# Attention head sums: PSUM leaves by ScalarE and is added on GpSimd in place of VectorE

## The chip, the cores and the metric

The kernel runs on one core of one Trainium2 chip. The metric is the device time of one execution in microseconds (us), median of several runs. Lower is better.

## What is computed

A post-norm transformer layer on x of shape (4, 1024, 128): causal attention with 8 heads of width 128 and rotary positions, then a gated feed-forward net with two further hidden layers. The part that matters here:

```python
q = rope(einsum('btm,mhd->bthd', x, w_aq))
k = rope(einsum('btm,mhd->bthd', x, w_ak))
v = einsum('btm,mhd->bthd', x, w_av)
s = einsum('bihd,bjhd->bhij', q, k) / 128      # masked where i < j
p = softmax(s, axis=-1)
o = einsum('bhij,bjhd->bihd', p, v)
r = einsum('bihd,hdm->bim', o, w_ao)           # the sum over heads
x = layernorm(x + r)
```

## The kernel before, in words

Output and value weights are multiplied together once, so that each head's weighted values are already its share of `r`, and the sum over the 8 heads of a batch entry is a plain sum into `rT`, a tile of 128 x 4096 in SBUF. There are 32 heads in all (4 batch entries of 8), taken in pairs; each head has 1024 tokens, that is 8 score blocks of 128 queries (`ib` 0 to 7, block `ib` having 128 x (ib + 1) columns) and 2 chunks of 512 tokens.

Float32 operands are split for TensorE into a high part and a low part, and each product is three matmuls. The low part is a subtraction on VectorE or GpSimd, after the high part has been rounded by a copy.

Each engine runs its own program, written out by hand as 8 steps for each head (the functions `step`), and the programs meet only through semaphores. Within an engine the order is fixed: an instruction that waits holds up all behind it. In step s of a head:

- TensorE makes the scores of block s + 2 (L391 to L395), transposes the normalised probabilities of block s (L404, s + 1 transposes), projects queries and keys of the next head in steps 0 and 2, values of the pair in steps 4 to 6 of the even head (L311), and multiplies probabilities by values (`attend`, L311): chunk 0 of this head in steps 6 and 7, chunk 1 of the **previous** head in steps 1, 2 and 3 (6, 6 and 12 matmuls). Both chunks use the one PSUM bank `pv_ps`.
- VectorE takes the reciprocal of the row sums of block s + 1 (L635), adds up rotated tiles (`rope_sum`, L660, two SBUF inputs), takes the negative maximum of block s + 2 (L629), adds a finished chunk of the previous head to `rT` (L678, `add_head`, chunk 0 in step 0, chunk 1 in step 4), and forms the low parts (L645, L665).
- ScalarE exponentiates block s + 1 (L525), rounds rotated tiles (L556), copies the transposed blocks of s (L537), copies projections out (L548) and rounds values (L563).
- GpSimd normalises the probabilities of block s + 1 (L720), multiplies swapped halves by the sine (L725, steps 1 to 4) and forms the low part of the rotated tiles (L732, steps 3, 4, 6 and 0).

`attend` may overwrite the bank only when the chunk before has been added (semaphore `pv_added`), and `add_head` waits for `pv_done`, the end of a chunk's products. A short queue of transfers on SyncE swaps the halves of projections. The feed-forward net follows after the attention part, at about 792 us.

Of the kernel before, what the change touches and what calls it, by code (L numbers as in the profile page):

```python
# [20 lines left out]
ACT = mybir.ActivationFunctionType  # L21
# [6 lines left out]
P = 128  # L28
# [27 lines left out]
V_STEP = (4, 5, 6, 6)  # L56
PV0_PIECES = {6: range(0, 2), 7: range(2, 4)}
PV1_PIECES = {1: range(0, 2), 2: range(2, 4), 3: range(4, 8)}
ADD0_STEP, ADD1_STEP = 0, 4
LEND1 = (6, 7, 0)  # L60
LEND3 = (1, 2)
FILLS_OF = [1 if i < 4 else 2 for i in range(NI)]
# [57 lines left out]
def attention(nc, ctx, sem, rT, ident, x_split, qk_split, v_split, xT, w_q, w_k, w_vT, w_o, rope_in, ident_in, mask_in,  # L120
              ffn_raw, ffn_weights, ffn_loaded):

    def sb(name, shape, dt=F32, where=ctx):
        return where.enter_context(nc.sbuf_tensor(name, shape, dt))
# [8 lines left out]
    proj = sb("proj", [P, 2, BANK])  # L133
    by_cos = sb("by_cos", [P, NQK, BANK])
    swapped = sb("swapped", [P, NQK, BANK])


    pre = ExitStack()
# [51 lines left out]
    v_high = (sem("v_high"), NV)  # L190
    v_low = (sem("v_low"), NV)
    pv_done = (sem("pv_done"), CHUNKS)
    pv_added = (sem("pv_added"), CHUNKS)
    swap_done = [(sem("swap_done0"), 64), (sem("swap_done1"), 64)]
    w_staged = [(sem("w_staged0"), 16), (sem("w_staged1"), 16)]
# [14 lines left out]
    def number(head):  # L210
        return 2 * head[0] + head[1]
# [7 lines left out]
    def exists(head):  # L219
        n = number(head)  # L220
        return not isinstance(n, int) or 0 <= n < HEADS

    def wait_for(eng, signal, head, nth):


        semaphore, each = signal
        if exists(head):
            eng.wait_ge(semaphore, each * number(head) + nth + 1)
# [9 lines left out]
    def earlier(head, nth, by, each):  # L238

        return step_on(head, (nth - by) // each), (nth - by) % each  # L240
# [33 lines left out]
    def is_first(head):  # L274
        return isinstance(head[0], int) and number(head) == 0
# [38 lines left out]
    with nc.Block() as block:  # L314
# [63 lines left out]
        def _(pe):  # L378
# [60 lines left out]
            def attend(head, chunk, key_blocks):  # L439

                if key_blocks[0] == 0:
                    wait_for(pe, t_low, head, NT - 1 if chunk else 3)
                    pair = head[0] + head[1] // 2
                    wait_for_pair(pe, v_low, pair, NV - 1 if chunk else 1)
                    wait_for(pe, pv_added, *earlier(head, chunk, 1, CHUNKS))
                for jb in key_blocks:
                    i0 = max(0, jb * P - chunk * BANK)
                    last = split_products(pv_ps[:, i0:], [vals[:, part, jb, parity(head)] for part in range(2)],
                                          [pT[chunk][:, part, jb, i0:] for part in range(2)],
                                          jb == 0, jb == 4 * chunk + 3)  # L450
                if key_blocks[-1] == 4 * chunk + 3:
                    last.then_inc(pv_done[0], 1)
# [30 lines left out]
        def _(act):  # L483
# [75 lines left out]
            def values_high(pair, nth):  # L559
                wait_for_pair(act, v_projected, pair, nth)  # L560
                if nth == 0:
                    wait_for(act, pv_done, (pair, -1), 1)
                nc.scalar.activation(vals[:, 0, 2 * nth:2 * nth + 2].rearrange("p j q m -> p (j q m)"),  # L563
                                     bank("v", 0, nth), ACT.Copy).then_inc(v_high[0], 1)

            def step(head, s, b):
                ahead = step_on(head, (s + 1) // NI)
                if before_first(head) and s == 1:
                    act.wait_ge(vo_ready, 1)
                    nc.scalar.activation(v_parts[:, 0], vo_ps, ACT.Copy).then_inc(vo_high, 1)  # L570
                if before_first(head) and s == 4:
                    for b in range(1, B):
                        high_of_x(b)
                if before_first(head) and s == NI - 2:
                    save_weights()
                if before_first(head) and s == NI - 1:
                    act.wait_ge(vo_low, 1)
                    act.wait_ge(x_low, B)
                    act.wait_ge(masks_ready, 1)
                if is_first(head) and s == NI - 1:  # L580
                    for b in range(2, B):
                        save_x(b)
                if is_first(head) and s == 4:
                    act.wait_ge(w_saved, W_SAVED)
                    act.wait_ge(wv_staged, 16)
                if exists(ahead):
                    exponentiate(ahead, (s + 1) % NI)
                for target, j in rope_tasks(head, s, HIGH_STEP):
                    roped_high(target, j)
                if exists(head):  # L590
                    transposed_high(head, s)
                for target, j in rope_tasks(head, s, QK_STEP):
                    copy_projected(target, j)
                for c in v_tasks(head, s):
                    values_high(head[0], c)
# [4 lines left out]
        def _(dve):  # L600
# [64 lines left out]
                nc.vector.tensor_tensor(low, bank("v", 0, nth), high.bitcast(F32),  # L665
                                        ALU.subtract).then_inc(v_low[0], 1)

            def add_head(head, chunk):

                if not exists(head):  # L670
                    return
                col = number(head) // H * T + chunk * BANK
                acc = rT[:, bass.ds(col, BANK)] if not isinstance(col, int) else rT[:, col:col + BANK]
                if is_first(head):
                    dve.wait_ge(r_zero, 1)
                wait_for(dve, pv_done, head, chunk)
                wait_for(dve, pv_added, *earlier(head, chunk, 2, CHUNKS))
                nc.vector.tensor_tensor(acc, pv_ps[:], acc, ALU.add).then_inc(pv_added[0], 1)  # L678

            def step(head, s, b):  # L680
                if before_first(head) and s == 3:
                    dve.wait_ge(vo_high, 1)
                    nc.vector.tensor_tensor(v_parts[:, 1], vo_ps, v_parts[:, 0].bitcast(F32),
                                            ALU.subtract).then_inc(vo_low, 1)
                    nc.vector.tensor_copy(ident_b[:], ident[:])
                    nc.vector.tensor_copy(mask_b[:], mask_f[:]).then_inc(masks_ready, 1)
                if before_first(head) and s == 5:
                    for b in range(1, B):
                        low_of_x(b)
                if exists(step_on(head, (s + 1) // NI)):  # L690
                    inverse_sum(step_on(head, (s + 1) // NI), (s + 1) % NI)
                for target, j in rope_tasks(head, s, SUM_STEP):
                    rope_sum(target, j)
                if exists(step_on(head, (s + 2) // NI)):
                    negative_max(step_on(head, (s + 2) // NI), (s + 2) % NI)
                if s == ADD0_STEP:
                    add_head(step_on(head, -1), 0)
                if s == ADD1_STEP:
                    add_head(step_on(head, -1), 1)
                if exists(head):  # L700
                    transposed_low(head, s)
                for target, j in rope_tasks(head, s, COS_STEP):
                    times_cos(target, j)
                for c in v_tasks(head, s):
                    values_low(head[0], c)
# [3 lines left out]
        @block.gpsimd  # L709
        def _(pool):  # L710
            nc.gpsimd.memset(warm[:], 0.0).then_inc(warm_zero, 1)
            nc.gpsimd.memset(rT[:], 0.0).then_inc(r_zero, 1)
            pool.wait_ge(consts_loaded, 48)

            def normalize(head, ib):
                n = parity(head) * NI + ib
                wait_for(pool, inv_ready, head, ib)
                pool.sem_inc(pool_passed, 1)
                p = probs[:, ib % 4, :(ib + 1) * P]
                nc.gpsimd.tensor_scalar(p, p, inv_sum[:, n:n + 1], 1.0, ALU.mult, ALU.mult).then_inc(probs_ready[0], 1)  # L720

            def times_sin(head, j):
                c = ROPE_TILES[j][1]
                wait_for_swap(pool, head, j)
                nc.gpsimd.tensor_tensor(swapped[:, j], swapped[:, j], rope[:, 1, c * BANK:(c + 1) * BANK],  # L725
                                        ALU.mult).then_inc(sin_done[0], 1)

            def roped_low(head, j):
                which, c = ROPE_TILES[j]
                high, low = (qk[:, parity(head), which, part, c * BANK:(c + 1) * BANK] for part in range(2))  # L730
                wait_for(pool, rope_high, head, j)
                nc.gpsimd.tensor_tensor(low, swapped[:, j], high.bitcast(F32), ALU.subtract).then_inc(rope_low[0], 1)  # L732

            def step(head, s, b):
                ahead = step_on(head, (s + 1) // NI)
                if exists(ahead):
                    normalize(ahead, (s + 1) % NI)
                for target, j in rope_tasks(head, s, SIN_STEP):
                    times_sin(target, j)
                for target, j in rope_tasks(head, s, LOW_STEP):  # L740
                    roped_low(target, j)

            run_pairs(pool, step)


# [456 lines left out]
```

## Time and profile before

| what | before |
|---|---|
| median of 3 runs | 1084.09 us (1081.2 to 1084.93) |
| the profiled execution, time | 1084.27 us |
| the profiled execution, span | 1082.5 us |
| TensorE busy | 1000.0 us (92%) |
| VectorE busy | 852.7 us (79%) |
| ScalarE busy | 657.0 us (61%) |
| GpSimd busy | 584.8 us (54%) |
| mean granted TensorE clock | 0.976 of full speed |

Busy shares are means over two parts that differ: GpSimd works almost only in the attention part, TensorE in both. To see what one more instruction costs, the timelines of the engines at the same place have to be laid beside each other.

### The profile page before, as it was taken

The numbers are of one execution on the slowest core, as the hardware profiler recorded it, in microseconds if no ns is written. First come the engines' busy times: TensorE is split into PE (matmuls) and PEld (weight loads), VectorE is DVE, ScalarE is ACT, GpSimd is POOL, SyncE is SP. The second block draws the span as 40 slices with busy tenths as digits, with TensorE's granted clock in tenths as the row PEclk, the third lists the DMA queues.
The fourth block names the chain that finished last, engine by engine and source line by source line (L and its number), as shares of the span: only waits on it lengthen the run. The fifth ranks groups of instructions, "written<-read, shape, count | busy, mean of one in ns | idle before, by whom it ended". The sixth has DMA issues, their size and how long they took to land. (4 is left out here: it accounts for less than half of the span.)

```text
span 1082.5 us, 20027 instructions
## 1 busy us (share of the span) xinstructions
PE 1000.0 (92%) x5648; PEld 829.6 (77%) x5648; DVE 852.7 (79%) x1803; ACT 657.0 (61%) x1383; POOL 584.8 (54%) x536
## 2 busy tenths in 40 slices
PE   2799999999999999999999999999929999999995
PEld 1588788878878888887888888787727878788784
DVE  4888888988878898897989888888755668486744
ACT  4577776777767777776767777677625252343531
POOL 3676777777767777777787776778450101000000
PEclk8899999999999999999999999999969999999998
DMA  7542223532222323222222223231020000000000
GB/s 247 166 137 60 63 63 87 156 88 59 59 60 67 78 58 88 59 61 67 68 67 58 50 59 73 59 80 42 1 79 1 1 1 21 0 19 0 1 20 20
DMA packets 33292, 66.16 MB, mean 61 GB/s; under 512 B 5456, under 2 KB 6992, under 8 KB 32208
## 3 DMA queue, kind: packets, MB, share of 16 engines
q1 hardware_dynamic: 30400, 58.62, 20.4%
q10 hardware_dynamic: 2832, 6.82, 1.7%
q8 instruction: 29, 0.48, 0.2%
q14 instruction: 31, 0.25, 0.1%
HBM read 24.26 MB, written 7.34 MB: 29 GB/s over the span
## 5 line engine op out<-in xcount | busy, mean ns | idle before, releaser
L720 POOL TENSOR_SCALAR probs<-probs,inv_sum 128x128 f32<-128x128 f32 (+7 forms) x256 | 236.2, 923 | 177.9 <-DVE inv_sum L635 177.9
L537 ACT ACTIVATE pT<-psum 128x512 fp32r<-128x512 f32 (+3 forms) x384 | 176.1, 490 | 129.8 <-PE psum L404 128.7
L311 PE MATMUL psum<-pT,vals 128*128 128x512 f32 (+3 forms) x1152 | 243.5, 351 | 1.6 <-DVE rT L678 1.6
L525 ACT ACTIVATE probs<-psum,neg_max 128x128 f32<-128x128 f32 (+7 forms) x256 | 190.5, 744 | 57.3 <-DVE neg_max L629 55.6
L645 DVE TENSOR_TENSOR pT<-psum,pT 128x512 fp32r<-128x512 f32 (+3 forms) x384 | 199.9, 547 | 15.1 <-ACT pT L537 12.0
L311 PEld LDWEIGHTS psum<-pT,vals 128*128 128x128 f32 x1152 | 188.9, 190 | 23.6 <-DVE pT L645 1.7
L629 DVE TENSOR_REDUCE neg_max<-psum 128x1 f32<-128x128 f32 (+7 forms) x256 | 190.4, 744 | 6.3 <-PE psum L395 6.3
L404 PE MATMUL psum<-ident,probs 128*128 128x128 f32 x1152 | 175.8, 278 | 15.0 <-POOL probs L720 7.6
L725 POOL TENSOR_TENSOR swapped<-swapped,rope 128x512 f32<-128x512 f32 x128 | 166.2, 1299 | 39.5 <-DMA swapped<-proj 38.6
L901 PE MATMUL ps<-hid,w 128*128 128x512 f32 x768 | 181.3, 396 | 0.0
L901 PEld LDWEIGHTS ps<-hid,w 128*128 128x128 f32 x768 | 143.7, 188 | 34.5
L732 POOL TENSOR_TENSOR qk<-swapped,qk 128x512 fp32r<-128x512 f32 x128 | 166.1, 1298 | 2.8 <-ACT qk L556 2.8
L404 PEld LDWEIGHTS psum<-ident,probs 128*128 128x128 f32 x1152 | 134.5, 141 | 42.1 <-DVE pT L645 13.1
L391 PE MATMUL psum<-qk 128*128 128x384 f32 (+5 forms) x384 | 136.7, 356 | 25.8 <-POOL qk L732 22.9
L660 DVE TENSOR_TENSOR swapped<-by_cos,swapped 128x512 f32<-128x512 f32 x128 | 123.1, 963 | 44.9 <-POOL swapped L725 44.9
L394 PE MATMUL psum<-qk 128*128 128x384 f32 (+5 forms) x384 | 151.3, 394 | 0.0
L395 PE MATMUL psum<-qk 128*128 128x384 f32 (+5 forms) x384 | 131.8, 343 | 0.0
L311 PE MATMUL psum<-x_moving,w_stage 128*128 128x512 f32 (+1 forms) x384 | 106.7, 414 | 9.9 <-DVEq L622 9.9
L995 ACT ACTIVATE value<-ps,scales 128x512 f32<-128x512 f32 x64 | 43.5, 690 | 96.9 <-PE ps L901 96.5
L391 PEld LDWEIGHTS psum<-qk 128*128 128x128 f32 x384 | 73.0, 190 | 36.0 <-issue 26.8
L1026 POOL COPY y<-y_norm 128x512 f32<-128x512 f32 (+1 forms) x8 | 5.2, 653 | 166.3 <-DVE y_norm L1083 166.3
L548 ACT ACTIVATE proj<-psum 128x512 f32<-128x512 f32 x128 | 75.2, 600 | 30.8 <-PE psum L311 26.1
(78 smaller groups left out, 1246.5 us busy)
## 6 DMA issues: line engine op xcount, KB each, us to landing
swapped<-proj SPq DMA_DIRECT2D x256, 128.0 KB, 2.3
w_stage<-qk_split SPq DMA_DIRECT2D x30, 256.0 KB, 2.7
wv_stage<-v_split SPq DMA_DIRECT2D x15, 256.0 KB, 2.6
x_split<-ffn_raw ACTq DMA_DIRECT2D x2, 1024.0 KB, 5.9
ffn_raw<-g SPq DMA_DIRECT2D x2, 1024.0 KB, 8.2
x_moving<-x_split SPq DMA_DIRECT2D x2, 1024.0 KB, 6.0
out<-y SPq DMA_DIRECT2D x4, 512.0 KB, 2.6
raw_x<-xT SPq DMA_DIRECT2D x3, 512.0 KB, 11.5
```

Of the source, the lines that this page charges most:

```text
L311: ins = nc.tensor.matmul(out_ap, left[a], right[b], start=first and i == 0, stop=last and i == 2)
L391: nc.tensor.matmul(dst, left[0], right[0], start=True, stop=False)
L394: nc.tensor.matmul(dst, left[0], right[1], start=False, stop=False)
L404: last = nc.tensor.transpose(bank("t", head[1], nth)[:, (jb % 4) * P:(jb % 4 + 1) * P], probs[:, ib % 4, jb * P:(jb + 1) * P], ident[:])
L525: nc.scalar.activation(probs[:, ib % 4, :width].rearrange("p (h c) -> p h c", h=halves), score_ps[:, ib % 2, :halves, :half], ACT.Exp, bia ...
L537: nc.scalar.activation(pT[chunk][:, 0, 4 * f:4 * f + n_blocks, (ib % 4) * P:(ib % 4 + 1) * P], bank("t", head[1], nth)[:, :n_blocks * P].r ...
L629: nc.vector.tensor_reduce(neg_max[:, n:n + 1], score_ps[:, ib % 2, :halves, :half], AX.XY, ALU.max, negate=True).then_inc(max_ready[0], 1)
L645: nc.vector.tensor_tensor(low, bank("t", head[1], nth)[:, :n_blocks * P].rearrange("p (j i) -> p j i", i=P), high.bitcast(F32), ALU.subtra ...
L720: nc.gpsimd.tensor_scalar(p, p, inv_sum[:, n:n + 1], 1.0, ALU.mult, ALU.mult).then_inc(probs_ready[0], 1)
L725: nc.gpsimd.tensor_tensor(swapped[:, j], swapped[:, j], rope[:, 1, c * BANK:(c + 1) * BANK], ALU.mult).then_inc(sin_done[0], 1)
L732: nc.gpsimd.tensor_tensor(low, swapped[:, j], high.bitcast(F32), ALU.subtract).then_inc(rope_low[0], 1)
L901: last = nc.tensor.matmul(ps[:, c, o], w_at(base, a, k * HID, o * P), hid[:, c, layer, b, k], start=k == 0 and i == 0, stop=k == HT - 1 an ...
```

## The change

The add into `rT` moves from VectorE to GpSimd. GpSimd cannot read the bank here, so ScalarE first copies `pv_ps` into a new SBUF tile `pv_stage` (128 x 512, one buffer). TensorE may overwrite the bank once the copy is done (`pv_staged`), and the copy waits until the add before it has read the stage.

```diff
-ADD0_STEP, ADD1_STEP = 0, 4
+STAGE_STEP = (0, 4)
...
+    pv_stage = sb("pv_stage", [P, BANK])
...
+    pv_staged = (sem("pv_staged"), CHUNKS)
...
-                    wait_for(pe, pv_added, *earlier(head, chunk, 1, CHUNKS))
+                    wait_for(pe, pv_staged, *earlier(head, chunk, 1, CHUNKS))
...
+            def stage_head(head, chunk):
+                wait_for(act, pv_done, head, chunk)
+                wait_for(act, pv_added, *earlier(head, chunk, 1, CHUNKS))
+                nc.scalar.activation(pv_stage[:], pv_ps, ACT.Copy).then_inc(pv_staged[0], 1)
...
+                if s in STAGE_STEP and exists(step_on(head, -1)):
+                    stage_head(step_on(head, -1), STAGE_STEP.index(s))
                 if exists(ahead):
                     exponentiate(ahead, (s + 1) % NI)
...
-                if s == ADD0_STEP:
-                    add_head(step_on(head, -1), 0)
-                if s == ADD1_STEP:
-                    add_head(step_on(head, -1), 1)
...
+            def add_head(head, chunk):
+                col = number(head) // H * T + chunk * BANK
+                acc = rT[:, bass.ds(col, BANK)] if not isinstance(col, int) else rT[:, col:col + BANK]
+                if is_first(head) and chunk == 0:
+                    pool.wait_ge(r_zero, 1)
+                wait_for(pool, pv_added, *earlier(head, chunk, 2, CHUNKS))
+                wait_for(pool, pv_staged, head, chunk)
+                nc.gpsimd.tensor_tensor(acc, pv_stage[:], acc, ALU.add).then_inc(pv_added[0], 1)
...
                 for target, j in rope_tasks(head, s, LOW_STEP):
                     roped_low(target, j)
+                if s in STAGE_STEP and exists(step_on(head, -1)):
+                    add_head(step_on(head, -1), STAGE_STEP.index(s))
```

On ScalarE, steps 3 to 5 of an odd head read as follows before (`probs` rows are the exponentials, `qk<-swapped` the rounding of a rotated tile, `pT` the copies of transposed blocks):

```order
L525 ACTIVATE probs,row_sum<-psum,neg_max 128x640
L556 ACTIVATE qk<-swapped 128x512
L537 ACTIVATE pT<-psum 128x4x128
L525 ACTIVATE probs,row_sum<-psum,neg_max 128x768
L556 ACTIVATE qk<-swapped 128x512
L537 ACTIVATE pT<-psum 128x4x128
L537 ACTIVATE pT<-psum 128x128
L525 ACTIVATE probs,row_sum<-psum,neg_max 128x896
```

With the change the same stretch of ScalarE, the line numbers of the changed file being a little higher, is:

```order
L527 ACTIVATE probs,row_sum<-psum,neg_max 128x640
L558 ACTIVATE qk<-swapped 128x512
L539 ACTIVATE pT<-psum 128x4x128
L571 ACTIVATE pv_stage<-psum 128x512
L527 ACTIVATE probs,row_sum<-psum,neg_max 128x768
L558 ACTIVATE qk<-swapped 128x512
L539 ACTIVATE pT<-psum 128x4x128
L539 ACTIVATE pT<-psum 128x128
L527 ACTIVATE probs,row_sum<-psum,neg_max 128x896
```

The copy of the finished bank stands directly ahead of the exponential of block 5 (128x768), and waits there for the previous head's last products.

On GpSimd, steps 3 to 6 of the same head read before (`probs` rows are normalisations, `swapped` the sine products, `qk<-swapped,qk` the low parts):

```order
L720 TENSOR_SCALAR probs<-probs,inv_sum 128x640
L725 TENSOR_TENSOR swapped<-swapped,rope 128x512
L732 TENSOR_TENSOR qk<-swapped,qk 128x512
L720 TENSOR_SCALAR probs<-probs,inv_sum 128x768
L725 TENSOR_TENSOR swapped<-swapped,rope 128x512
L732 TENSOR_TENSOR qk<-swapped,qk 128x512
L720 TENSOR_SCALAR probs<-probs,inv_sum 128x896
```

With the change, the same stretch of GpSimd is:

```order
L713 TENSOR_SCALAR probs<-probs,inv_sum 128x640
L718 TENSOR_TENSOR swapped<-swapped,rope 128x512
L725 TENSOR_TENSOR qk<-swapped,qk 128x512
L713 TENSOR_SCALAR probs<-probs,inv_sum 128x768
L718 TENSOR_TENSOR swapped<-swapped,rope 128x512
L725 TENSOR_TENSOR qk<-swapped,qk 128x512
L734 TENSOR_TENSOR rT<-pv_stage,rT 128x512
L713 TENSOR_SCALAR probs<-probs,inv_sum 128x896
```

The add stands between the low part of the second rotated tile and the normalisation of block 6 (128x896).

## Rows read from the trace of the kernel before

**Rows 1.** Busy time by windows: from:to, us, busy (instructions), granted clock, DMA, GB/s

```profile
core 0: us, PE busy (x) PEld busy (x) DVE busy (x) ACT busy (x) POOL busy (x), PEclk, DMA share, GB/s
60.00:780.00 720.00, 698.65 (x4276) 587.05 (x4275) 621.28 (x1221) 513.97 (x1159) 529.03 (x487) 1.00 0.27 69
```

**Rows 2.** Waits of TensorE, 100 to 780 us: total, times, longest

```profile
PE psum L391 <- POOL qk L732: 9.5, 14, 0.7
PE psum L404 <- POOL probs L720: 4.9, 15, 0.4
PE psum L404 <- DVE pT L645: 4.8, 14, 0.7
```

**Rows 3.** Timeline of TensorE, head 15: start, duration, instructions, idle before

```profile
400.60 2.11 PE L311 MATMUL psum<-pT,vals 128*128 128x512 f32 x12
...
407.95 0.32 PE L391 MATMUL psum<-qk 128*128 128x128 f32 x1 [0.70 <-POOL qk L732]
...
408.87 0.98 PE L404 MATMUL psum<-ident,probs 128*128 128x128 f32 x7 [0.30 <-POOL probs L720]
```

**Rows 4.** Timeline of TensorE, head 16 and the start of 17

```profile
423.12 2.11 PE L311 MATMUL psum<-pT,vals 128*128 128x512 f32 x12
...
431.25 1.05 PE L404 MATMUL psum<-ident,probs 128*128 128x128 f32 x7
...
442.44 0.49 PE L404 MATMUL psum<-ident,probs 128*128 128x128 f32 x3
```

**Rows 5.** Timeline of ScalarE, head 16

```profile
424.09 0.90 ACT L525 ACTIVATE probs<-psum,neg_max 128x768 f32<-128x768 f32 x1
...
427.92 0.60 ACT L563 ACTIVATE vals<-psum 128x512 fp32r<-128x512 f32 x1
428.42 1.00 ACT L525 ACTIVATE probs<-psum,neg_max 128x896 f32<-128x896 f32 x1
```

**Rows 6.** Timeline of GpSimd, heads 15 and 16 and the start of 17

```profile
403.99 1.35 POOL L720 TENSOR_SCALAR probs<-probs,inv_sum 128x768 f32<-128x768 f32 x1
...
407.79 1.02 POOL L720 TENSOR_SCALAR probs<-probs,inv_sum 128x896 f32<-128x896 f32 x1
...
426.35 1.34 POOL L720 TENSOR_SCALAR probs<-probs,inv_sum 128x768 f32<-128x768 f32 x1
...
430.18 1.01 POOL L720 TENSOR_SCALAR probs<-probs,inv_sum 128x896 f32<-128x896 f32 x1
...
440.82 0.59 POOL L720 TENSOR_SCALAR probs<-probs,inv_sum 128x384 f32<-128x384 f32 x1 [0.94 <-DVE inv_sum L635]
```

**Rows 7.** Timeline of VectorE, head 16

```profile
425.19 1.72 DVE L660 TENSOR_TENSOR swapped<-by_cos,swapped 128x512 f32<-128x512 f32 x1
```

**Rows 8.** Groups by line, whole span: busy us, mean ns, idle before

```profile
L725 POOL TENSOR_TENSOR swapped<-swapped,rope 128x512 f32<-128x512 f32 x128 | 166.2, 1299 | 39.5 <-DMA swapped<-proj 38.6 <-DVE inv_sum L635 0.8
L548 ACT ACTIVATE proj<-psum 128x512 f32<-128x512 f32 x128 | 75.2, 600 | 30.8 <-PE psum L311 26.1 <-DMA swapped<-proj 2.5 <-issue 0.3
L678 DVE TENSOR_TENSOR rT<-psum,rT 128x512 f32<-128x512 f32 x64 | 43.4, 678 | 5.0 <-PE psum L311 5.0
```

**Rows 9.** Timeline of three engines in head 31, where GpSimd only normalises

```profile
773.97 0.90 ACT L525 ACTIVATE probs<-psum,neg_max 128x768 f32<-128x768 f32 x1
...
775.00 0.16 DVE L635 RECIPROCAL inv_sum<-row_sum 128x1 f32<-128x1 f32 x1 [0.26 <-ACT probs L525]
775.36 0.91 POOL L720 TENSOR_SCALAR probs<-probs,inv_sum 128x768 f32<-128x768 f32 x1 [2.34 <-DVE inv_sum L635]
```

**Rows 10.** Groups by form, GpSimd, 100 to 780 us: block 4

```profile
L720 POOL TENSOR_SCALAR probs<-probs,inv_sum 128x640 f32<-128x640 f32 x29 | 30.3, 1044 | 29.9 <-DVE inv_sum L635 29.9
```

**Rows 11.** Groups by form, GpSimd, 765 to 785 us: block 4 in head 31

```profile
L720 POOL TENSOR_SCALAR probs<-probs,inv_sum 128x640 f32<-128x640 f32 x1 | 0.8, 809 | 2.1 <-DVE inv_sum L635 2.1
```

**Rows 12.** Busy time by windows, columns as in rows 1

```profile
310.00:313.50 3.50, 1.72 (x10) 0.81 (x8) 3.50 (x7) 1.97 (x4) 3.50 (x4) 1.00 0.00 0
313.50:317.50 4.00, 3.98 (x16) 3.57 (x17) 3.37 (x9) 3.16 (x7) 3.00 (x3) 0.57 0.01 2
78.00:82.00 4.00, 4.00 (x19) 3.51 (x18) 2.29 (x7) 1.89 (x7) 2.99 (x3) 0.57 0.01 2
```

More of the change, by code:

```diff
@@ L666, in values_low @@
                                         ALU.subtract).then_inc(v_low[0], 1)
[L668 to L678, printed above, removed]
             def step(head, s, b):
```

## The prediction

> **What bounds the kernel now.** I read the busy time by windows first. In the attention part, from 60 to 780 us, TensorE is busy 698.65 of 720 us [rows 1] at the full granted clock of 2.4 GHz, VectorE 621.28, GpSimd 529.03 and ScalarE 513.97. TensorE's instruction stream is the bound; every stall put into it lengthens the run one for one, and only some 21 us of idle are there to win. The waits of TensorE [rows 2] say what it stalls on: the low part of the rotated keys and queries (L732) and the normalised probabilities (L720), both made by GpSimd. So GpSimd, only 73% busy, sets the few stalls there are, because it works in order.
>
> The timelines show where. Number the heads 0 to 31; heads 15 and 16 show the two patterns, since the values of a pair are projected in its even head. In head 15 the transposes of score block 6 (x7) start at 408.87 after a wait of 0.30 us for GpSimd [rows 3], and the normalisation they wait for ran from 407.79 for 1.02 [rows 6]: 0.06 us from its end to their start. In head 16 the transposes start at 431.25 with no wait, and that normalisation ended at 430.18 + 1.01 = 431.19 [rows 4, 6]: the same 0.06 us. At this place, once in each head, GpSimd has no slack. Elsewhere it has: block 2's normalisation begins at 440.82 after 0.94 us of idle and is wanted 1.03 us after its end (440.82 + 0.59 against 442.44) [rows 4, 6].
>
> **The change part by part.**
>
> Removed: 64 VectorE adds of 0.678 us, 43.4 us [rows 8]. They are hidden work, apart from the last one of all: TensorE never waits for VectorE's total, only for single results. I put the gain at nothing. The cover is TensorE's own stream; without it the bound of the gain would be the 43.4 us.
>
> Added on ScalarE: 64 copies of 128x512 out of PSUM, like L548 at 0.600 us [rows 8]. From such a copy to the next start it is 0.50 us (427.92 to 428.42) [rows 5]. Total work is no matter (514 of 720 us); what matters is the place. In step 4 the copy stands **ahead of** the exponential of block 5 and waits for the end of the previous head's twelve second-chunk products. In head 16 these end at 423.12 + 2.11 = 425.23 [rows 4], while the exponential had started at 424.09 [rows 5]. So the exponential now starts at 425.23 + 0.50 = 425.73. Queued behind it on ScalarE are the rounding of the rotated tile (L556) and the copies of the transposes; VectorE's reciprocal waits for the exponential, GpSimd's normalisation for the reciprocal.
>
> From the exponential of block 5 to its reciprocal and on to the normalisation takes 773.97 to 775.00 to 775.36, so 1.03 + 0.36 us [rows 9]. Normalisation 5 then starts at 427.12 instead of 426.35 [rows 6]. How long it takes there the trace doesn't show directly. It takes 1.34 now; undisturbed 0.91 [rows 6, 9]. Today VectorE's two-input add L660 waits 425.19 to 426.9 behind a GpSimd tile and then runs across the normalisation's start [rows 7]. Afterwards the add follows its reciprocal at once, as it now does at block 4, where the normalisation takes 1.044 against 0.809 undisturbed [rows 10, 11]. I take 0.91 + 0.24 = 1.15, with 0.91 and 1.34 as ends. It ends at 428.27, where it ended at 427.69: 0.58 late.
>
> The Trainium skill (SBUF — State Buffer, "SBUF: two separate sides") says that GpSimd and a VectorE instruction with two SBUF inputs exclude each other for a whole instruction, the first to start winning. By it the added GpSimd work could also hold up L660; at step 4 no L660 is due while the add runs, so by the page the sum would stay as it is.
>
> Added on GpSimd: 64 adds of two SBUF operands, like L725 at 1.30 us [rows 8], same shape, types and engine, so I take that; the ends are 0.68, what VectorE took for the sum, and 1.72, a two-input instruction that found the other engine in its way [rows 7, 8]. At step 4 the add stands between the rotation work and normalisation 6, which had no slack. Normalisation 6 therefore ends 0.58 + 1.30 = 1.88 us later in head 16, and TensorE's transposes with it.
>
> In head 15, the same: products end at 400.60 + 2.11 = 402.71, exponential 403.21, normalisation 404.60 to 405.75, where it was 403.99 to 405.34 [rows 3, 6]: 0.41 + 1.30 = 1.71 us. The 1.2 us of waits that TensorE has there already don't cover it, since the transposes' start itself moves; the key tile of L732 comes only 0.41 later and lies inside the same stretch.
>
> After the stall everything upstream has caught up, because TensorE alone is late, so the next head pays again. At step 0 the same pair of edits costs nothing: the copy waits for products that end about when the exponential started, at most 0.56 late, and 0.56 + 1.30 minus 0.94 of idle is 0.92, under the 1.03 of slack.
>
> The count: head 0 has no predecessor and head 31 no rotation work on GpSimd, so heads 1 to 30 pay: 15 x (1.88 + 1.71) = 53.9 us. At the very end the last sum goes through 0.60 + 1.30 instead of 0.68 us: 1.2 us. Together 55.
>
> **The clock.** In the attention part the granted clock is 2.4 GHz except for two short falls to 1.2 GHz, at 78 and at 313 us. Before the one at 313 TensorE was busy 1.72 of 3.50 us, in just the stretch of an odd head that I lengthen, and the fall gave a mean of 0.57 over 4 us, a loss of 4 x 0.43 = 1.7 us; the other was the same [rows 12]. So one fell after 1.78 us of idle; the odd heads, with 0.70 + 0.30 + 1.71 = 2.7 us of it [rows 3], will do so more often. By how much no row says: the ends are no further fall and one in each of the 28 heads that have none now (48 us). I take nine of the 15 odd heads, seven more than now, 12 us.
>
> The Trainium skill (TensorE: Matmul & The Clock Gate, "Why this matters for your kernels") warns only of longer single gaps than any that I expect here; by it the clock would hold and the time be 1139. The trace disagrees: no single wait before the fall at 313 was over 0.70 us.
>
> Sum: the profiled execution took 1084.27 us, beside a span of 1082.5 and a median of 1084.09, so I use 1084.3. 1084.3 + 55 + 12 = **1151 us**.
>
> **The rivals.**
>
> 1. The stall as above, the clock falling in some odd heads only: 1151, chance 0.45.
> 2. The stall without further falls: 1139, chance 0.20. For it: single gaps stay under 2 us. Against it: [rows 12].
> 3. The clock falls in nearly every head: 1139 + 48 = 1187, chance 0.11. Even heads have a single gap of 1.9 us, which speaks against it.
> 4. Only one of the two delays binds: the add's 1.30 but not the held exponential, since GpSimd is busy until about that time anyway: 30 x 1.3 + 1 = 40, so 1124, chance 0.15. It would need GpSimd to reach normalisation 5 when it does now.
> 5. Faster: GpSimd has 191 us of idle in the 720, the adds need 83. If the add fell into that idle, ahead of normalisation 5, VectorE's relief would shorten TensorE's waits for the low parts (L645, 4.8 us, and a share of the rest in [rows 2]) to give about 1077. It decides at the 0.06 us of slack found above: the add must cost normalisation 6 less than that. Its place in the order speaks against it. Chance 0.04.
> 6. Both cancel or all is hidden, 1084: chance 0.05.
>
> Numbers: differences under 0.3% can't be told from none in this kernel; faster 0.04, same 0.05, slower 0.91. Lower ends (no falls, normalisation 0.24 shorter in 30 heads, 7 us) give 1132, the fourth rival 1124; upper ends (all odd heads fall, 22 us in place of 12, normalisation 0.19 longer, 6 us) give 1167, and beyond lies the third rival. The range of 8 in 10 is 1125 to 1172.
>
> **What would show it.** In the changed profile: VectorE without the 43 us; TensorE waiting for L720's successor at the x7 transposes by some 1.5 to 2 us in each head, at no other place by much; normalisation 5 starting 0.6 to 0.8 us later after the x12 products than now; the add between the last rotation tile and normalisation 6; heads longer by 1.7 to 1.9 us in the undisturbed case, more where the granted clock falls. Wrong would make me: an exponential of block 5 that isn't held, waits of TensorE at block 2 or 5 instead, or the clock.

## The result, and the profile after

The changed kernel takes 1154.93 us (median of 4 runs, 1153.83 to 1156.06) against 1082.64 us for the kernel before beside it. The ratio is 1.069, 95% interval 1.067 to 1.072. The forecast was 1151 us, range 1125 to 1172. The profiled execution took 1153.83 us.

The head of the page of the changed kernel (busy us, share of the span, instructions):

```profile
PE 1022.8 (89%) x5648; PEld 850.4 (74%) x5648; DVE 802.9 (70%) x1739; ACT 691.2 (60%) x1447; POOL 662.4 (58%) x600
```

VectorE gave up 49.8 us, and GpSimd took on 77.6. The attention part, now about 70 us longer, with the columns of [rows 1]:

```profile
60.00:850.00 790.00, 721.81 (x4281) 608.12 (x4280) 573.99 (x1160) 547.75 (x1224) 604.51 (x549) 0.96 0.24 63
```

TensorE is idle for 68.2 us of it, where it was 21.4 [rows 1], and its mean granted clock has fallen from 1.00 to 0.96. The waits of TensorE from 100 to 840 us, beside [rows 2]:

```profile
PE psum L406 <- POOL probs L713: 45.0, 30, 1.6
PE psum L393 <- POOL qk L725: 17.7, 14, 1.3
```

L713 is the normalisation (L720 before), L725 now the low part of the rotated tiles (L732 before). The wait for the normalisation went from 4.9 to 45.0 us. TensorE's timeline of heads 15 and 16, beside [rows 3, 4], shows where:

```profile
431.09 2.11 PE L313 MATMUL psum<-pT,vals 128*128 128x512 f32 x12
...
438.90 0.32 PE L393 MATMUL psum<-qk 128*128 128x128 f32 x1 [1.28 <-POOL qk L725]
...
441.04 1.75 PE L406 MATMUL psum<-ident,probs 128*128 128x128 f32 x7 [1.52 <-POOL probs L713]
...
456.73 2.11 PE L313 MATMUL psum<-pT,vals 128*128 128x512 f32 x12
...
466.72 0.98 PE L406 MATMUL psum<-ident,probs 128*128 128x128 f32 x7 [1.59 <-POOL probs L713]
...
477.80 0.49 PE L406 MATMUL psum<-ident,probs 128*128 128x128 f32 x3
```

From the end of the twelve products to the x7 transposes it is 441.04 - 433.20 = 7.84 us in head 15 and 466.72 - 458.84 = 7.88 in head 16. Before it was 6.16 and 6.02. I call this distance the **gap** below. In nearly every head from 2 to 29 of this kernel it is 7.83 to 7.89 us, whatever came before: a chain that starts at the products sets it. ScalarE's and GpSimd's timelines of head 16 are that chain (beside [rows 5, 6]):

```profile
458.88 0.60 ACT L571 ACTIVATE pv_stage<-psum 128x512 f32<-128x512 f32 x1 [1.27 <-PE psum L313]
459.37 0.90 ACT L527 ACTIVATE probs<-psum,neg_max 128x768 f32<-128x768 f32 x1
```

```profile
460.76 1.18 POOL L713 TENSOR_SCALAR probs<-probs,inv_sum 128x768 f32<-128x768 f32 x1 [0.69 <-DVE inv_sum L644]
461.91 1.29 POOL L718 TENSOR_TENSOR swapped<-swapped,rope 128x512 f32<-128x512 f32 x1
463.17 1.28 POOL L725 TENSOR_TENSOR qk<-swapped,qk 128x512 fp32r<-128x512 f32 x1
464.41 1.26 POOL L734 TENSOR_TENSOR rT<-pv_stage,rT 128x512 f32<-128x512 f32 x1
465.66 2.54 POOL L713 TENSOR_SCALAR probs<-probs,inv_sum 128x896 f32<-128x896 f32 x2
...
476.79 0.59 POOL L713 TENSOR_SCALAR probs<-probs,inv_sum 128x384 f32<-128x384 f32 x1
```

ScalarE sat idle for 1.27 us in front of the copy, since the copy waits for the products; the exponential of block 5 stands behind it. On GpSimd the add (L734) comes after the low part, and normalisation 6 (128x896, the first of the merged x2) starts only when it ends. The reader can add up 458.84, 458.88, 459.37, 460.76, 465.66 and 466.72 and meets no slack anywhere.

The clock, in windows of heads 15 and 16:

```profile
437.00:441.00 4.00, 1.17 (x7) 0.69 (x6) 3.29 (x8) 3.14 (x7) 4.00 (x5) 0.96 0.00 0
441.00:445.00 4.00, 3.96 (x18) 3.56 (x18) 1.95 (x5) 1.44 (x4) 3.14 (x3) 0.61 0.00 0
455.00:467.00 12.00, 10.40 (x69) 8.72 (x68) 9.91 (x20) 9.07 (x19) 10.34 (x10) 1.00 0.49 155
467.00:471.00 4.00, 4.00 (x33) 3.77 (x31) 3.05 (x8) 2.53 (x6) 2.69 (x3) 1.00 0.16 28
```

In head 15 TensorE is busy for 1.17 of 4 us and then runs at 1.2 GHz for most of the next 4: the seven transposes take 1.75 us, in head 16 0.98. Windows of 1 us over the whole attention part show 17 such falls, in 13 of the 15 odd heads that pay and in 4 of the even ones, and each takes 1.7 us of full-speed time away, as in [rows 12]. The profile before has two.

### The profile page after: what moved, and what is told of

Read it like the earlier page. It is cut to its first block and busy times, and to the rows that moved or that the text cites. A ratio compares the mean times of both kernels' runs of the same rounds, so it can differ in the third digit from the quotient of the medians.

```text
span 1152.0 us, 20131 instructions
## 1 busy us (share of the span) xinstructions
PE 1022.8 (89%) x5648; PEld 850.4 (74%) x5648; DVE 802.9 (70%) x1739; ACT 691.2 (60%) x1447; POOL 662.4 (58%) x600
## 5 line engine op out<-in xcount | busy, mean ns | idle before, releaser
L713 POOL TENSOR_SCALAR probs<-probs,inv_sum 128x128 f32<-128x128 f32 (+7 forms) x256 | 235.1, 920 | 190.2 <-DVE inv_sum L644 189.1
L313 PE MATMUL psum<-pT,vals 128*128 128x512 f32 (+3 forms) x1152 | 256.3, 365 | 0.9 <-DVE pT L654 0.9
L406 PE MATMUL psum<-ident,probs 128*128 128x128 f32 x1152 | 179.8, 283 | 51.8 <-POOL probs L713 49.0
L313 PEld LDWEIGHTS psum<-pT,vals 128*128 128x128 f32 x1152 | 198.9, 199 | 25.0 <-DVE pT L654 1.1
L406 PEld LDWEIGHTS psum<-ident,probs 128*128 128x128 f32 x1152 | 139.4, 144 | 76.2 <-POOL probs L713 56.7
L725 POOL TENSOR_TENSOR qk<-swapped,qk 128x512 fp32r<-128x512 f32 x128 | 166.3, 1299 | 2.8 <-ACT qk L558 2.8
L669 DVE TENSOR_TENSOR swapped<-by_cos,swapped 128x512 f32<-128x512 f32 x128 | 100.4, 785 | 42.5 <-POOL swapped L718 42.5
L644 DVE RECIPROCAL inv_sum<-row_sum 128x1 f32<-128x1 f32 x256 | 40.6, 159 | 100.3 <-ACT probs L527 99.1
```

The source lines that it names most:

```text
L313: ins = nc.tensor.matmul(out_ap, left[a], right[b], start=first and i == 0, stop=last and i == 2)
L406: last = nc.tensor.transpose(bank("t", head[1], nth)[:, (jb % 4) * P:(jb % 4 + 1) * P], probs[:, ib % 4, jb * P:(jb + 1) * P], ident[:])
```

## The experiments

Theory: two delays add up in each head, the exponential of block 5 held behind the copy (0.4 to 0.6 us) and the add ahead of normalisation 6 (1.3 us), and the longer idle stretch makes the clock fall. Rivals: only one of the two binds; GpSimd's whole load, or its contention with VectorE, costs the time wherever the add stands; the clock's falls cost nothing.

**Each delay alone, both away, and the add without VectorE's relief.** Four kernels on one chip, beside 8 runs of the kernel before (1079.5 us).

The copy behind the exponential:

```diff
-                if s in STAGE_STEP and exists(step_on(head, -1)):
-                    stage_head(step_on(head, -1), STAGE_STEP.index(s))
                 if exists(ahead):
                     exponentiate(ahead, (s + 1) % NI)
+                if s in STAGE_STEP and exists(step_on(head, -1)):
+                    stage_head(step_on(head, -1), STAGE_STEP.index(s))
```

> The changed kernel with ScalarE's copy of the bank moved behind the exponential of the same step, the GpSimd add left where it is. Theory (two delays add up: the held exponential is worth 0.4 to 0.6 us a head, the add ahead of normalisation 6 1.3 us): from the end of the twelve products to the x7 transposes 7.4 to 7.5 us in place of 7.86, 30 x 0.4 = 12 us less, about 1142 us, the clock still falling in about half of the heads. Rival (only the add counts, the hold is hidden behind GpSimd's own work): no difference, 1155.

Measured: 1132.21 us (1130.74 to 1136.25), ratio to before 1.049 (1.046 to 1.051). The gap is 7.22 to 7.43 us in 21 of the 30 heads and longer in the others. GpSimd's timeline:

```profile
427.65 1.35 POOL L713 TENSOR_SCALAR probs<-probs,inv_sum 128x768 f32<-128x768 f32 x1
...
431.43 1.28 POOL L734 TENSOR_TENSOR rT<-pv_stage,rT 128x512 f32<-128x512 f32 x1
432.68 2.54 POOL L713 TENSOR_SCALAR probs<-probs,inv_sum 128x896 f32<-128x896 f32 x2
```

No wait is left ahead of normalisation 5, and it has its old length of 1.35 again. The hold was real. The loss beside the kernel before fell from 72.3 to 52.7 us, by 20 us where 12 were expected. Between the two profiled executions (1153.83 and 1136.25 us) it is 17.6: the gaps of heads 1 to 30 add up to 225.5 us in place of 236.0, 10.5 less (0.35 a head), and the clock falls 12 times in place of 17.

The add behind normalisation 6:

```diff
+ADD_STEP = (0, 5)
...
-                if s in STAGE_STEP and exists(step_on(head, -1)):
-                    add_head(step_on(head, -1), STAGE_STEP.index(s))
+                if s in ADD_STEP and exists(step_on(head, -1)):
+                    add_head(step_on(head, -1), ADD_STEP.index(s))
```

> The changed kernel with GpSimd's add of chunk 1 moved behind the normalisation of block 6 (step 5 in place of step 4), ScalarE's copy left ahead of the exponential. Theory: products to x7 transposes 6.6 us in place of 7.86, so 30 x 1.28 = 38 us less, and the clock falls seldom again, up to 20 us more: 1097 to 1116 us. Rival (GpSimd's whole load or contention with VectorE costs the time, not the place of the add): the add still takes 1.3 us of a busy engine, no more than 10 us less, 1145 or above.

Measured: 1100.09 us (1097.24 to 1102.37), ratio 1.019 (1.016 to 1.022). The gap is 6.61 to 6.66 us in nearly every head, and the clock falls twice. The hold shows in GpSimd's timeline, ahead of normalisation 5, and TensorE's shows what is left of the stall:

```profile
482.93 1.18 POOL L714 TENSOR_SCALAR probs<-probs,inv_sum 128x768 f32<-128x768 f32 x1 [0.59 <-DVE inv_sum L645]
...
486.58 1.02 POOL L714 TENSOR_SCALAR probs<-probs,inv_sum 128x896 f32<-128x896 f32 x1
487.56 1.29 POOL L735 TENSOR_TENSOR rT<-pv_stage,rT 128x512 f32<-128x512 f32 x1
```

```profile
487.66 0.98 PE L407 MATMUL psum<-ident,probs 128*128 128x128 f32 x7 [0.29 <-POOL probs L714]
```

GpSimd does the same work as in the changed kernel; only one instruction changed places, and the loss beside the kernel before fell from 72 to 21 us. Load and contention as such are out.

Both edits together:

> Both edits at once: copy behind the exponential, add of chunk 1 behind normalisation 6. Theory: both delays are gone and the stall is that of the kernel before, 6.0 to 6.2 us from products to x7 transposes: 1076 to 1086 us. If VectorE's relief of 43 us were of use to TensorE, the time would come out well under 1076. Rival (load or contention): above 1110.

Measured: 1084.41 us (1082.54 to 1086.57), ratio 1.005 (1.003 to 1.007). The gap is 6.04 to 6.19 us in most heads. So nearly the whole loss was the places of two instructions. What is left, 5 us, is slower than before beyond the interval. TensorE's timeline of head 15 has a wait that the kernel before has not, ahead of the x8 transposes:

```profile
406.06 0.32 PE L394 MATMUL psum<-qk 128*128 128x128 f32 x1 [1.12 <-POOL qk L726]
...
406.97 0.98 PE L407 MATMUL psum<-ident,probs 128*128 128x128 f32 x7 [0.29 <-POOL probs L714]
...
409.83 1.09 PE L407 MATMUL psum<-ident,probs 128*128 128x128 f32 x8 [0.19 <-POOL probs L714]
```

From 100 to 780 us TensorE's waits for VectorE's low parts (`pT`) have gone from 4.8 us [rows 2] to 0.2, so the relief of VectorE does reach TensorE. But the low part made by GpSimd comes no earlier, and TensorE waits for that instead: 15.2 us in place of 9.5, and 11.0 for the normalisations in place of 4.9. The relief of 43 us is worth nothing in time even here. Which wait makes the last 5 us isn't shown.

The kernel before, with a useless GpSimd add at the end of step 4 and VectorE's adds left in place:

```diff
+                if s == 4 and exists(step_on(head, -1)):
+                    pool.wait_ge(extra_zero, 1)
+                    wait_for(pool, extra_done, step_on(head, -2), 0)
+                    nc.gpsimd.tensor_tensor(extra[:, 2], extra[:, 0], extra[:, 1], ALU.add).then_inc(extra_done[0], 1)
```

> The kernel before, VectorE keeping its adds, with one further GpSimd add of two 128x512 SBUF tiles of no use at the end of step 4 of each head but the first. The output is unchanged. Theory (the add's place is what costs, VectorE's work costs nothing): as the kernel with only the add's delay, 7.4 us from products to x7 transposes, about 1140 us, within 5 us of the run with the copy behind the exponential. Rival (VectorE's relief has already paid back part of the loss in the changed kernel): 10 us or more above that run.

Measured: 1133.98 us (1133.08 to 1135.61), ratio 1.051 (1.048 to 1.053); 12 falls of the clock, and a median gap of 7.35 us in odd and 7.42 in even heads. GpSimd's timeline:

```profile
430.82 1.27 POOL L748 TENSOR_TENSOR extra<-extra 128x512 f32<-128x512 f32 x1
432.07 2.53 POOL L723 TENSOR_SCALAR probs<-probs,inv_sum 128x896 f32<-128x896 f32 x2
```

This is 1.8 us from the run with the copy behind the exponential. One unneeded instruction of 1.27 us in each head, of no use to anyone and on an engine 73% busy, costs 54 us, and VectorE's relief pays back next to nothing. The two runs differ in ScalarE's copies and GpSimd's add of chunk 0 as well, so a small gain of the relief that these use up isn't ruled out.

**The clock by itself.** The changed kernel, TensorE filling its wait with small matmuls:

```diff
+FILLER = 14
...
+                if ib == 6:
+                    wait_for_banks(pe, head[0], "t", head[1], FIRST_FILL[ib])
+                    for _ in range(FILLER):
+                        nc.tensor.matmul(bank("t", head[1], FIRST_FILL[ib])[:, :P], ident_b[:], ident_b[:], start=True,
+                                         stop=True)
                 wait_for(pe, probs_ready, head, ib)
...
-                    wait_for_banks(pe, head[0], "t", head[1], nth)
+                    if ib != 6 or f:
+                        wait_for_banks(pe, head[0], "t", head[1], nth)
```

> The changed kernel, with 14 small bf16 matmuls without use (identity by identity, 128x128) on TensorE while it waits for normalisation 6, into the bank that the transposes overwrite afterwards. Theory (17 clock falls cost the changed kernel 1.3 to 1.7 us each, and come from the idle stretch): few falls are left, products to x7 transposes stay at 7.8 to 8.0 us, time 1155 less 15 x 1.3 = 20 us, about 1135. Rival (the falls cost nothing since the next stall takes them in, or don't hang on this idle time): 1153 to 1160.

Measured: 1144.86 us (1143.84 to 1147.23) beside a kernel before of 1079.3, ratio 1.060 (1.057 to 1.063), where the changed kernel had 1.069. Between the two medians lie 10 us. Between the two profiled executions, 1153.83 and 1147.23 us, lie 6.6, and the falls went from 17 to 12: 1.3 us for each. TensorE's timeline of two neighbouring heads:

```profile
434.25 0.32 PE L394 MATMUL psum<-qk 128*128 128x128 f32 x1 [1.29 <-POOL qk L732]
434.71 0.96 PE L405 MATMUL psum<-ident_b 128*128 128x128 bf16 x14
436.40 1.76 PE L413 MATMUL psum<-ident,probs 128*128 128x128 f32 x7 [0.73 <-POOL probs L720]
...
460.21 0.96 PE L405 MATMUL psum<-ident_b 128*128 128x128 bf16 x14
461.97 0.98 PE L413 MATMUL psum<-ident,probs 128*128 128x128 f32 x7 [0.81 <-POOL probs L720]
```

The gap stayed at 7.85 to 7.99 us in nearly every head, so the time went with the falls. No even head falls any more, but 12 odd heads do: they keep the other wait of 1.29 us ahead of the scores, which wasn't filled. The rival that the falls are taken in by the next stall is out; a third to a half of the 20 us expected came, because only some of the falls went.

**Looking for a faster version.** If GpSimd's order in step 4 sets what is left of TensorE's waits, its last sine product could go behind normalisation 6 too (`SIN_STEP = (1, 2, 3, 5)` in place of `(1, 2, 3, 4)`), on top of both edits and, on its own, in the kernel before.

> The run with both edits moved, and besides GpSimd's last sine product (L725, fourth tile) moved from step 4 behind normalisation 6 in step 5, ahead of the add. Theory (GpSimd's order in step 4 sets TensorE's remaining waits): the odd heads' waits for the low part and for normalisation 6, 1.0 us together, shrink to 0.3 or less and even heads gain 0.2: 12 to 20 us less than with both moved, 1065 to 1073 us. Rival (VectorE's reciprocal or the next rotation tile is late instead): within 5 us of it.

> The kernel before with only that sine product moved to step 5, VectorE keeping its adds. Theory: it gains 8 to 15 us as well, 1065 to 1072 us; if VectorE's add ahead of the reciprocal of block 6 is the next bound, it gains less than the run with everything moved, which then is at least 3 us faster than this one. Rival: VectorE's relief is of no use even there, and this one is as fast or faster.

Measured: 1094.02 us (1092.85 to 1094.68), ratio 1.013 (1.011 to 1.015), and 1078.06 us (1077.09 to 1078.73), ratio 0.998 (0.997 to 0.999). Both are beside a kernel before of 1079.3 us. In the first, a gain was expected and a loss came. TensorE's timeline of head 15 shows normalisation 6 earlier, a gap of 5.48 us in place of 6.15, and the stall back one place later:

```profile
411.90 0.99 PE L407 MATMUL psum<-ident,probs 128*128 128x128 f32 x7 [0.80 <-POOL probs L714]
416.02 1.09 PE L407 MATMUL psum<-ident,probs 128*128 128x128 f32 x8 [1.43 <-POOL probs L714]
```

Sine product and add together, 2.6 us, stand ahead of normalisation 7, which has room for about one of them. In the kernel before, where only one moves, the gain is 0.2% and not the 8 to 15 us expected. The gap in odd heads did shrink, to a median of 5.57 us from 6.12, and the 9.5 us of waits for the low part [rows 2] are gone, but TensorE waits 16.0 us for the normalisations from 100 to 780 us, where it was 4.9 [rows 2]: a part of the stall has only moved. It is the fastest version of this study, and it needs nothing of the change.

Two further attempts from the run with both edits moved, beside a kernel before of 1079.99 us. VectorE takes the low part of the second rotated tile, in step 4 where its add had stood (counted by a semaphore `rope_low_v`), or the add of chunk 1 goes to step 7 (`ADD_STEP = (0, 7)`):

```diff
                 for target, j in rope_tasks(head, s, LOW_STEP):
-                    roped_low(target, j)
+                    if j != 1:
+                        roped_low(target, j)
...
+                for target, j in rope_tasks(head, s, LOW_STEP):
+                    if j == 1:
+                        high, low = (qk[:, parity(target), 1, part, :BANK] for part in range(2))
+                        wait_for(dve, rope_high, target, j)
+                        nc.vector.tensor_tensor(low, swapped[:, j], high.bitcast(F32),
+                                                ALU.subtract).then_inc(rope_low_v[0], 1)
```

> The run with both edits moved, and besides the low part of the second rotated tile (L732, 1.3 us of GpSimd) taken by VectorE in step 4, where its add had stood, counted by a semaphore of its own. GpSimd's stretch ahead of normalisation 6 gets 1.3 us shorter, VectorE pays 0.7 us or, if it finds GpSimd in its way, up to 1.9. Theory (GpSimd's order in step 4 sets the odd heads' waits of 1.0 to 1.4 us): half to all of them go, 8 to 18 us less than with both moved, 1066 to 1076 us, faster than before. Rival (VectorE is then late with the reciprocal of block 6): no gain, 1080 to 1095.

> The run with both edits moved, but the add of chunk 1 in step 7, behind the normalisation of the next head's block 0. Theory (the 5 us by which that run is above the kernel before come from the add ahead of normalisation 7): they go, within 3 us of the kernel before. Rival (the copy on ScalarE costs them): no difference to the run with both moved.

Measured: 1116.79 us (1113.69 to 1118.87), ratio 1.034 (1.032 to 1.036), worse than either expectation, and 1094.36 us (1091.66 to 1097.81), ratio 1.012 (1.010 to 1.014), where neither had expected a loss. For the first, VectorE's timeline of one head:

```profile
392.87 1.08 DVE L644 TENSOR_REDUCE neg_max<-psum 128x1 f32<-128x896 f32 x1
393.87 1.65 DVE L703 TENSOR_TENSOR qk<-swapped,qk 128x512 fp32r<-128x512 f32 x1
395.45 0.88 DVE L660 TENSOR_TENSOR pT<-psum,pT 128x512 fp32r<-128x512 f32 x2
```

and TensorE's at the same place:

```profile
396.18 0.87 PE L409 MATMUL psum<-ident,probs 128*128 128x128 f32 x6 [0.88 <-DVE pT L660]
```

The subtraction has two SBUF inputs and takes 1.65 us where VectorE's add out of PSUM took 0.68 [rows 8]; the low part of the transposes (L660) comes a microsecond late, and TensorE waits for that instead: 29.6 us in all from 100 to 780 us. The 10 us that the add in step 7 costs on top of both edits I didn't resolve. GpSimd's timeline there has it start at 395.75, ahead of a normalisation and a low part. But TensorE's waits from 100 to 780 us add up to the same 26.4 us as with both edits moved. What differs is the clock: it falls 7 times in this profile and not at all in the other, which at 1.7 us each is up to 12 us. Why it falls here, although the waits are no longer in sum, stays open.

## Why the prediction was right, point by point

- **No gain from VectorE's 43 us.** Right, and shown two ways: two runs that differ in the relief lie 1.8 us apart, and with both edits moved there is no gain either.
- **The held exponential.** Forecast 0.50 us from copy to exponential and normalisation 5 starting 1.89 us after the products; measured 459.37 - 458.88 = 0.49, and 460.76 - 458.84 = 1.92. Its length, which no row showed, was put at 1.15 and is 1.18. As forecast, VectorE's two-input add (L660, now L669) follows its reciprocal at once and still lies across the normalisation's start, by 0.40 us where it was 0.56 (425.19 + 1.72 - 426.35):

```profile
460.47 0.69 DVE L669 TENSOR_TENSOR swapped<-by_cos,swapped 128x512 f32<-128x512 f32 x1
```

- **The add ahead of normalisation 6.** Forecast 1.30; from its start to the next it is 1.25. Both together were to lengthen the gap by 1.88 in head 16 and 1.71 in head 15; measured 1.86 and 1.68. The 0.06 us of slack was the point that decided, as the fifth rival had it, and it decided against it.
- **Step 0 costs nothing.** Right: normalisation 2 ends at 476.79 + 0.59 = 477.38, the transposes start at 477.80 without a wait. Of 1.03 us of slack 0.42 are left, where the forecast left 0.11; its "at most 0.56 late" rested on no row shown.
- **The count.** The even heads pay less than head 16, on average: their gap before was mostly 6.17 to 6.21, so 1.7 us each in both kinds, and 30 x 1.7 = 51 us in place of 53.9. A few heads of the kernel before had longer gaps of their own (6.5 to 7.3, some 4 us together), which the chain now covers. All gaps of heads 1 to 30 add up to 236.0 us after 188.7: 47 us. The 1.2 us for the last sum hardly show: from head 31's transposes of block 6 (780.52 and 849.72) to the end of the span it is 302.0 us before and 302.3 now.
- **The clock.** This is the term that was mis-sized. Nine falls were taken, 17 came, 4 of them in even heads; net of the two before that is 15 x 1.7 = 25 us against 12. The mechanism was right in the main: the falls follow the idle stretch, and where it is shorter they go (17, 12, 2 over the changed kernel and the runs with one delay away). What decides whether one head has a fall no run shows: with the add in step 7 the clock falls 7 times behind waits that cause no fall with both edits moved. The two delays add up: the add alone costs about 53 us, the hold alone 21, both 72 beside kernels before of 1080 to 1083. In time a fall costs less than 1.7: the two heads from 13 to 15 took 46.6 us before and 51.4 now with one fall among them, 4.8 us, of which 3.4 are the gaps and so 1.4 the fall. The 47 us of gaps, 0.3 at the end and 15 falls of 1.4 to 1.5 give 68 to 70 us against a measured 1153.83 - 1084.27 = 69.6.
- **Luck in the total.** The terms for the two delays and the end were 55 us and came to 48, the clock's was 12 and came to about 22. The two errors go opposite ways, so that the total is closer than its terms.
- **The rivals.** Only one delay binding: out, each edit alone gives its own part. The time without falls, 1139, was out as well. The Trainium skill (TensorE: Matmul & The Clock Gate, "Why this matters for your kernels") warns of single gaps between bursts of matmuls that are longer than any here; this case's trace disagrees, since the clock fell with single waits of 1.28 and 1.52 us and TensorE busy for 1.17 of the 4 us before.

## What to carry to other kernels

Before moving work to an engine with idle time, ask what stands behind it in that engine's order, and how long before its deadline that ends: here an engine 73% busy had 0.06 us, and one place later about a microsecond (an add of 1.27 us there left TensorE a wait of 0.19). A copy that frees a bank should not stand ahead of an instruction on the critical chain if it waits for something later than that instruction does. And a stall of TensorE can cost more than its own length, if the clock falls after it.

## What the runs showed of the hardware that I had not expected

- The clock fell although no single wait of TensorE was over 1.6 us: 17 times in the changed kernel, each fall taking 1.7 us of full-speed time. The kernel with the add in step 7 had 7 falls with no wait over 1.3 us.
- A VectorE subtraction with two SBUF inputs (the run with the low part on VectorE) took 1.63 to 1.67 us in the 31 of 32 instances beside GpSimd's work, and 0.69 in the one without it. The add with one input in PSUM took 0.67 to 0.69 us all 64 times in the kernel before, 61 of them beside GpSimd's work, so it was never held up. This agrees with the exclusion told of in the Trainium skill (SBUF — State Buffer, "SBUF: two separate sides").
